# Flamingo-style cross attention and FP4 feed-forward layer on one core: set-up calls reordered on four engines, third sequence's scores moved to the end of the set-up, row gathers one step sooner

## The reference, cut to what matters

```python
# x: (8, 256, 256)   ctx_2048: (8, 64, 256)   token_to_sets: (256, 4)
def _L0_xattn_ref(token_states, set_states, desc_router, W_q, b_q, token_to_sets):
    q = jnp.einsum('bsd,ed->bse', token_states, W_q) + b_q
    scores = jnp.einsum('bse,ne->bsn', q, desc_router) * scale
    scores = jnp.where(mask[None, :, :], scores, neg_inf)     # 4 allowed sets of 64 per token
    topk_vals, topk_idx = jax.lax.top_k(scores, 2)
    weights = softmax over the two picks
    return jnp.einsum('bsn,bnd->bsd', weights, set_states)

def _L0_ffn_ref(x, ...):                                      # 2048 hidden units
    Wg, Wu, Wd = dequant_nvfp4(gate), dequant_nvfp4(up), dequant_nvfp4(down)
    gate = xt @ Wg.T;  up = xt @ Wu.T
    gelu = jnp.tanh(0.7978845608028654 * (gate + 0.044715 * gate ** 3)) * gate * 0.5 + gate * 0.5
    return (gelu * up) @ Wd.T

x = x + tanh(g_xattn) * _L0_xattn_ref(_layernorm(x), ctx_2048, ...)
x = x + tanh(g_ffn) * _L0_ffn_ref(_layernorm(x), ...)
```

## Time and profile before

| | before |
|---|---|
| median of 3 runs | 311.27 us (311.02 to 311.34) |
| the profiled execution's own time | 311.26 us |
| its span, first to last instruction | 309.5 us |
| TensorE busy | 302.0 us, 98% of the span |
| VectorE busy | 223.6 us, 72% |
| ScalarE busy | 155.9 us, 50% |
| GpSimd busy | 144.8 us, 47% |
| granted TensorE clock | 1.0 in every stretch |

### The profile page before, as it was taken

How to read it: one execution, slowest core, us unless ns; L and a number is a source line. 1 busy time by engine, 2 the same in 40 slices (tenths; PEclk the granted TensorE clock), 3 DMA queues, 4 the chain that set the end, 5 groups by cost and what they waited for, 6 DMA issues and landing times.

```text
span 309.5 us, 4648 instructions
## 1 busy us (share of the span) xinstructions
PE 302.0 (98%) x1537; PEld 251.0 (81%) x1537; DVE 223.6 (72%) x478; ACT 155.9 (50%) x287; POOL 144.8 (47%) x138
## 2 busy tenths in 40 slices
PE   6998999999999999999999999999999999999996
PEld 4777888787788788888888888888888888888885
DVE  3999999899985669687676678777676565544545
...
GB/s 184 253 186 0 150 124 0 0 37 1 0 2 0 2 34 17 77 57 123 70 101 3 17 17 26 94 53 85 63 94 0 0 15 26 26 40 0 37 0 68
DMA packets 47288, 16.11 MB, mean 52 GB/s; under 512 B 38944, under 2 KB 44448, under 8 KB 47264
## 3 DMA queue, kind: packets, MB, share of 16 engines
...
...
## 4 chain that ended last, share of the span: by engine, by line
PE 78%; issue 7%; POOL 6%; DVE 4%; ACT 2%; DMA 2%; SPq 0%; DVEq 0%; POOLq 0%
PE ring_ps L1317 49%; PE acc_ps L1351 17%; PE acc_ps L1364 4%; PE att_ps L1364 3%; POOL act_lo L525 3%; POOL w_nat L507 2%; DMA x_sb<-in_x_dram 2%; PE att_ps L1219 1%; POOL w_nat L518 1%; PE ring_ps L1302 1%; ACT act L695 1%; DVE act L1006 0%; DVE act L1000 0%; DVE x_sb L1157 0%; ACT act L691 0%
## 5 line engine op out<-in xcount | busy, mean ns | idle before, releaser
L525 POOL TENSOR_TENSOR act_lo<-act,act_hi 128x512 fp32r<-128x512 f32 x63 | 82.1, 1302 | 118.8 <-ACT act_hi L702 118.6
L1317 PE MATMUL ring_ps<-xt_hi,w_hi 128*128 128x512 f32 (+1 forms) x264 | 103.8, 394 | 1.0 <-ACT xt_hi L675 0.7
L1317 PE MATMUL ring_ps<-xt_hi,w_lo 128*128 128x512 f32 (+1 forms) x264 | 100.9, 384 | 0.0
L1317 PE MATMUL ring_ps<-xt_lo,w_hi 128*128 128x512 f32 (+1 forms) x264 | 100.2, 384 | 0.0
L691 ACT ACTIVATE act<-ring_ps 128x512 f32<-128x512 f32 x64 | 38.1, 596 | 84.2 <-PE ring_ps L1317 83.8
L1000 DVE SCALAR_TENSOR_TENSOR act<-act,ring_ps 128x512 f32<-128x512 f32 x64 | 43.7, 683 | 39.1 <-ACT act L691 38.9
L1006 DVE SCALAR_TENSOR_TENSOR act<-act,ring_ps 128x512 f32<-128x512 f32 x64 | 43.8, 685 | 27.2 <-ACT act L695 25.9
L1317 PEld LDWEIGHTS ring_ps<-xt_hi,w_hi 128*128 128x128 f32 x264 | 49.7, 188 | 11.1 <-issue 1.2
L1317 PEld LDWEIGHTS ring_ps<-xt_lo,w_hi 128*128 128x128 f32 x264 | 49.0, 188 | 10.3 <-DVE xt_lo L938 0.2
L695 ACT ACTIVATE act<-act 128x512 f32<-128x512 f32 x64 | 40.5, 632 | 32.7 <-DVE act L1000 32.7
L1317 PEld LDWEIGHTS ring_ps<-xt_hi,w_lo 128*128 128x128 f32 x264 | 49.8, 188 | 8.3
...
## 6 DMA issues: line engine op xcount, KB each, us to landing
...
ln_dram<-normed SPq DMA_DIRECT2D x16, 64.0 KB, 2.2
w_nat<-ln_dram SPq DMA_DIRECT2D x16, 64.0 KB, 2.0
...
```

What stands on the lines that cost most here:

```text
L525: pool.tensor_tensor(act_lo[:, s % RING, :], act[:, s % ACT_RING, :], act_hi[:, s % RING, :].bitcast(F32), ALU.subtract).then_inc(inter_lo, 1)
L1317: i = pe.matmul(into[:, tok], wt[:, n, w], xt[:, c % 2, k, tok], start=(k, j) == order[0], stop=(k, j) == order[-1])
```

## The change

It reorders calls of the set-up on TensorE, VectorE, ScalarE and GpSimd. `score(CB)` is called at the set-up's end, and no longer in step 2 of the main loop. In `LATER_STEPS` the entry ATTEND is 3 in place of 4 and 6 in place of 7. No arithmetic changes, and the loads are issued in the same order. `first_products` and `second_products` are helpers that hold the body of the loops they replace.

```diff
-    LATER_STEPS = ((0, 0, 1, 2, 3, 4, 6, 8, 12, 12), (3, 3, 4, 5, 6, 7, 9, 11, 15, 15))
+    LATER_STEPS = ((0, 0, 1, 2, 3, 3, 6, 8, 12, 12), (3, 3, 4, 5, 6, 6, 9, 11, 15, 15))
...
             root_2(1)
-            for i in range(2):
-                scale_rows_of(1, i)
+            scale_rows_of(1, 0)
+            scale_rows_of(1, 1)
+            root_1(CB)
             scale_down_of(1)
-            root_1(CB)
...
             x_t_out(1)
+            compact(0)
             lead_out(0)
-            compact(0)
...
+            compact(1)
             probs_out(0)
             lead_out(1)
+            rows_high(0)
+            normalise(0)
             sc.wait_ge(down_scales_loaded, 16)
             sc.activation(scales_sb[:, :, 4:6, :].rearrange("p r a b -> p a r b"), down_scales_sb[:, :, :, :],
                           ACT.Copy).then_inc(down_scales_placed, 1)
-            compact(1)
-            rows_high(0)
-            normalise(0)
             probs_out(1)
...
             square(1)
+            rows_high(3)
             tanh(1)
-            rows_high(3)
...
             find_where(0)
+            unpack(0, 0)
             weigh(0)
             input_variance(1)
-            for stage in range(3):
-                unpack(0, stage)
+            unpack(0, 1)
+            unpack(0, 2)
             read_scores(1)
             find_top(1)
-            find_lead(1)
             update_stats(0)
             update_variance(0)
+            find_lead(1)
             find_where(1)
             find_shift(0)
             weigh(1)
+            unpack(1, 0)
             rows_low(0)
-            unpack(1, 0)
             unpack(1, 1)
...
-            down_tile_low(0)
             turn_blocks(CB)
             input_stats(CB)
+            down_tile_low(0)
             ln2_low(1)
+            unpack(2, 0)
             input_variance(CB)
-            for stage in range(3):
-                unpack(2, stage)
+            unpack(2, 1)
             cubic(0)
             rows_low(2)
+            unpack(2, 2)
             gated_of(0)
             cubic(1)
             inter_of(0)
             gated_of(1)
+            inter_of(1)
             rows_low(3)
-            inter_of(1)
...
             score(1)
+            turn_probs(0)
             warm(2)
-            turn_probs(0)
             warm(4)
             attend_first(0)
+            warm(4)
             add_x(1)
             warm(4)
             turn_tile(0)
             turn_tile(1)
-            warm(4)
             turn_probs(1)
             turn_normed(0)
             attend_first(1)
+            turn_tile(2)
+            first_products("gate", 0)
+            first_products("up", 0)
+            first_products("gate", 1)
             turn_normed(1)
+            first_products("up", 1)
+            second_products("gate", 0, gate_done)
+            turn_tile(3)
             turn_tile(4)
+            second_products("up", 0, up_done)
+            second_products("gate", 1, gate_done)
+            second_products("up", 1, up_done)
+            score(CB)
...
                     for b in next_sequences(c, n, SCORE):
-                        score(b)
+                        if b > CB:
+                            score(b)
```

24 lines of the change are left out of this document (9 added, 15 removed).

## The result

| | before | after |
|---|---|---|
| median of the runs beside each other | 311.14 us | 313.71 us (313.41 to 314.16) |
| ratio | | 1.0083, 95% interval 1.0066 to 1.0101 |
| profiled execution, its span | 311.26, 309.5 | 313.68, 311.9 |
| granted clock | 1.0 | 0.999 |
| VectorE busy | 223.6 us | 229.3 us |

The change makes the kernel slower by 0.8%. The forecast was 310.9 us with a range up to 311.6; the result lies outside.

The account below looks back on a forecast made before the run. TensorE's stream was taken to bound the main loop, so only its idle time before that counts. Terms of -0.35, 0, 0 and 0 us took the profiled 311.26 to a forecast 310.9 us, range 310.3 to 311.6.

Parts of the forecast that it names:

- Term 1: End of set-up: the scores' new place and VectorE's new order let the gate of unit 3 start 0.35 us earlier.
- Two of its signs: Expected in the profile after: gate of unit 2 right behind the scores, and no idle before `cubic(2)`.
- Term 2: Set-up, start of the second halves on TensorE at 25.37: change 0, bounds -0.49 and +0.3 us.
- sequence 1 also gains: Rival, set-up: the second halves' start gives 0.3 to 0.49 us as well, 310.4 to 310.6; chance 0.27.
- The two things that were to delay the shift: Set-up: the down scales' copy (0.29) right before `probs_out(1)`, and four fillers before tile 0, delaying sequence 1's shift.
- Term 3: Set-up, first sequence's choice: `compact(1)` ahead of `probs_out(0)` hides by 0.07 us; change 0.
- the rival of the late load: Set-up: `compact(1)` waits for its load and holds `probs_out(0)`, each microsecond beyond 12.57 paid one for one; chance 0.10.
- Term 4: Main loop, gathers one step sooner: `low_part` behind `add_output` can come about 1 us later, covered; change 0.
- TensorE doesn't wait for VectorE in that stretch: Main loop, chunks 1 and 2: why VectorE losing its idle 0.57 for the gathered rows was counted as 0.
- a power beside L968: Rival, set-up: GpSimd's `root_1(2)` excludes VectorE's L968, up to 0.69 us before `cubic(0)`, 311.6; chance 0.02.
- The chance of slower: Whole kernel above 311.89 us: 0.08, two thirds of the late load and little else.
- The sum's base: Whole kernel: profiled execution's 311.26 and the runs' median 311.27 taken as the same, so the forecast starts there.

Follow-up runs that it names:

- e4: Changed kernel with only the second sequence's gather a step sooner (6), the first back at its old step 4; 314.16 us, ratio to before 1.0097.
- e12: Kernel with the new set-up and the gathers' old steps, but VectorE's set-up in the order of before; 310.31 us, ratio to before 0.9991.
- e2: Kernel before, old set-up, with only the gathers' new steps; 314.05 us, ratio to before 1.0095.
- e1: Changed kernel with the gathers back at their old steps, so only the set-up is new; 310.53 us, ratio to before 0.9983.
- f1: Kernel before, unchanged, profiled a second time; first turn of x at 5.87, gate of unit 3 at 34.79; no median given.
- f2: Kernel before, unchanged, profiled a third time; first turn of x at 6.19, gate of unit 3 at 35.11; no median given.
- e7: Changed kernel with the four L892 row adds reading one tensor instead of two; one run took 312.12 us.
- e6: Changed kernel with GpSimd's add of the stored sequence cut from 512 elements of each partition to 2; one run took 310.2 us.

## Why the prediction was wrong

**Term 1, scores and VectorE's order, -0.35: too large.** Between the second halves and the gate of unit 3, the stretch that the term is about, the kernel gains 0.13 (10.54 to 10.41). Two of its signs came: the gate of unit 2 starts right behind the scores, and `cubic(2)` has no idle. But "it gains the idle 0.35 and no more" left out that L974 had filled a wait. Without it VectorE stands idle 0.43 for `square(0)` (timeline of VectorE, after), where it had no idle before:

```profile
26.18 0.69 DVE L1000 SCALAR_TENSOR_TENSOR act<-act,ring_ps 128x512 f32<-128x512 f32 x1 [0.43 <-ACT act L691]
```

**Term 2, the second halves, 0: too small.** Measured from `probs_out(0)` they start 0.36 sooner (11.96 to 11.60). It is the rival "sequence 1 also gains": `normalise(1)` no longer stands behind L615, and starts 0.19 behind its shift (22.07 and 21.88) where it had started 0.55 behind (23.17 and 22.62). The two things that were to delay the shift cost nothing: it comes 9.21 behind `probs_out(0)`, 9.22 before.

**Term 3, the first sequence's choice, 0: the rival of the late load took place.** `compact(1)` waited for its load, 0.54, and `probs_out(0)` started right behind it (timeline of ScalarE, after):

```profile
11.92 0.84 ACT L602 ACTIVATE code_bytes<-packed 128x768 uint8<-128x768 uint8 x1 [0.54 <-DMA packed<-L_ffn_down_W_packed_dram]
12.67 0.45 ACT L641 ACTIVATE probs_t<-acc_ps,half_gate 64x256 f32<-64x256 f32 x1
```

Against the first turn of x that is 0.22 later than before, and it is paid almost one for one, as the rival said: `probs_out(0)` at 6.64 (after), 6.83 (e4) and 7.06 (e12) has the second halves at 18.23, 18.43 and 18.67.

So the set-up's 0.28 is 0.13 + 0.36 - 0.22, within the rounding. That it lies near the forecast 0.35 is luck: three terms were off and cancelled.

**Term 4, the gathers one step sooner, 0: this step failed.** It said that the `low_part` behind `add_output` comes about 1 us later and that this is covered, since the result is read one step on. Both were right: L525 stands at 135.42 where it stood at 135.50, in a loop that runs 1.17 ahead. `add_output` itself got no number. The two issues of a call took 2.33 with their gaps (131.83 to 134.16), and L542, which began 1.36 ahead of `add_rows` before, began 1.32 behind its start, 2.7 later in all. What I didn't price was the neighbour on the other engine: a GpSimd instruction moved in time is also a hold on VectorE moved in time. The runs put 3.0 us (e2 against before) to 3.6 us (e4 against e1) on it, in the changed kernel in four pieces of 0.7 to 1.05. The two pieces of 1.05, from the holds of 3.35, are in no profile without it; holds of 1.5 are in the kernel before as well in some executions. "TensorE doesn't wait for VectorE in that stretch" was true of before and put no number on the slack: 2.87 of hold came and 1.05 was paid at steps 25 and 26, so there is room for some 1.8 us of VectorE's delay there.

**The rivals.** The only slower ones were a late load and a power beside L968, both in the set-up. The first came, in small, and was outweighed by what sequence 1 gained. The second didn't: L968 took 0.36 at 25.39 beside the power of 25.56. But it had the right mechanism, a lock between VectorE and GpSimd, at the wrong place, with 0.02. The rows that would have placed it were in the trace of before: L849 and L925 up to 0.83 and 0.48 where their least is 0.16 and 0.15, and L968 at 1.09 three times beside L518, against L1006 at 0.69 throughout. The chance of slower, 0.08, should have held the whole of the gathers' part, for which the forecast had no rival.

**The sum's base.** "The median of the runs is the same within 0.01" was chance, as f1 and f2 show.

What stays open: the third L892 of the changed kernel would have ended at 134.13, and L542's record begins at 134.18, yet it was held. In e7 it would have ended at 134.15 and L542's record begins at 134.49. In e6 an L892 that ended at 134.64 was free, though `low_part` begins at 134.66. I can't say when GpSimd takes the port. Whether the 1.5 us hits of sequences 5 and 7 follow from the landing alone isn't shown either.
